# Second cross-attention: the key stack copied in two sides, its maxima found over four groups of a quad

## What is computed

```python
qn = layernorm(q, norm_w, norm_b)
kn = layernorm(k, norm_w, norm_b)
vn = layernorm(v, norm_w, norm_b)
Q = (qn @ Wq + bq).reshape(b, l, H, E)        # b 16, l 64, H 16 heads, E 16
K = (kn @ Wk + bk).reshape(b, s, H, E)        # s 1601
V = (vn @ Wv + bv).reshape(b, s, H, E)
scores = jnp.einsum('blhe,bshe->bhls', Q, K)
A = jax.nn.softmax(scale * scores, axis=-1)
O = jnp.einsum('bhls,bshd->blhd', A, V) + Q
```

## Time and profile before

| | before |
|---|---|
| median of three runs | 1640.6 us (1639.12 to 1641.78) |
| profiled execution | 1641.75 us, span 1640.0 us |
| PE, DVE, ACT, POOL busy | 88%, 61%, 40%, 39% of the span |
| mean granted clock of PE | 0.895 of full |
| the attention's 32 quads | about 582 to 1376 us of the span |

### The profile page before, as it was taken

One profiled execution on the slowest core, in us unless ns is written; L12 is line 12 of the kernel. 1 busy time (PEld: TensorE's weight loads), 2 busy tenths in 40 slices (PEclk: granted clock), 3 DMA queues, 4 the chain that ended last, 5 costly groups with the idle time before them and its releaser, 6 DMA issues. The chain is left out here.

```text
span 1640.0 us, 29797 instructions
## 1 busy us (share of the span) xinstructions
PE 1450.6 (88%) x11472; PEld 1148.9 (70%) x11472; DVE 995.0 (61%) x1896; ACT 655.0 (40%) x1268; POOL 641.6 (39%) x559
## 2 busy tenths in 40 slices
PE   6988877765994899999999999999999997489998
PEld 3655545444884678888888888888888875357787
DVE  4999964476236556666666666666665652644445
ACT  1444432131200455555545555545555533143322
POOL 0000000001001458777777777787776642222110
PEclk9877788866996899999999999999999985699999
DMA  9479700800142566766657767658666451311000
GB/s 358 157 276 326 266 2 1 298 2 0 59 148 89 139 159 164 188 158 161 158 144 180 173 158 168 150 144 197 169 150 143 98 109 26 107 39 64 0 1 27
DMA packets 109296, 219.61 MB, mean 134 GB/s; under 512 B 10871, under 2 KB 83095, under 8 KB 108391
## 3 DMA queue, kind: packets, MB, share of 16 engines
q1 hardware_dynamic: 109163, 217.80, 47.6%
HBM read 132.51 MB, written 6.40 MB: 85 GB/s over the span
## 5 line engine op out<-in xcount | busy, mean ns | idle before, releaser
L1905 DVE TENSOR_REDUCE d_top<-psum 128x1 f32<-128x400 f32 (+2 forms) x512 | 270.2, 569 | 97.7 <-PE psum L1549 90.5
L1449 POOL TENSOR_TENSOR d_ring<-d_ring 128x512 f32<-128x512 f32 x224 | 290.6, 1297 | 78.8 <-ACT d_ring L1734 61.1
L1734 ACT ACTIVATE d_ring<-psum 128x512 f32<-128x512 f32 (+1 forms) x416 | 229.2, 595 | 207.3 <-PE psum L1567 189.0
L1567 PEld LDWEIGHTS psum<-d_queries,d_stack 100*128 100x128 f32 (+1 forms) x1664 | 214.5, 198 | 36.7 <-issue 34.7
L1567 PE MATMUL psum<-d_queries,d_stack 100*128 100x128 f32 (+1 forms) x1664 | 235.9, 286 | 0.9 <-DVE d_queries L1920 0.9
L1549 PE MATMUL psum<-d_stack,d_queries 96*128 96x400 f32 (+1 forms) x512 | 171.8, 394 | 13.0 <-DVE d_top L1905 10.5
L1379 POOL TENSOR_TENSOR d_rowsT<-d_raw,d_rowsT 128x768 fp32r<-128x768 f32 (+2 forms) x62 | 118.2, 1908 | 156.2 <-ACT d_rowsT L1705 156.2
L1534 PE MATMUL psum<-d_wv,d_rowsT 128*128 128x256 f32 (+1 forms) x1248 | 169.9, 285 | 0.0
L1526 PE MATMUL psum<-d_rowsT,d_wk 128*128 128x384 f32 (+2 forms) x768 | 160.5, 358 | 3.5 <-POOL d_rowsT L1379 1.9
L1534 PEld LDWEIGHTS psum<-d_wv,d_rowsT 128*128 128x128 f32 (+1 forms) x1248 | 161.4, 187 | 0.5 <-issue 0.5
L973 POOL TENSOR_TENSOR c_partL<-moe_in,c_partH 128x256 fp32r<-128x256 f32 x8 | 5.5, 742 | 389.6 <-ACT c_partH L1061 389.6
(11 more groups left out here) (394 smaller groups left out, 2292.6 us busy)
## 6 DMA issues: line engine op xcount, KB each, us to landing
d_stack<-d_stage SPq DMA_DIRECT2D x384, 200.2 KB, 4.2
a_cR<-ctx_rows_dram SPq DMA_DIRECT2D x16, 1664.0 KB, 9.6
a_cT<-ctxT_dram SPq DMA_DIRECT2D x16, 1601.0 KB, 14.4
moe_w<-moe_w_dram SPq DMA_DIRECT2D x16, 1024.0 KB, 10.6
d_rowstd<-row_stds_dram SPq DMA_DIRECT2D x16, 801.0 KB, 5.5
d_raw<-ctxT_dram SPq DMA_DIRECT2D x32, 384.0 KB, 5.7
d_raw<-ctxT_dram SPq DMA_DIRECT2D x16, 512.0 KB, 6.0
d_queries<-queries_dram SPq DMA_DIRECT2D x96, 64.0 KB, 2.0
```

The source lines that it names most:

```text
L1449: pool.tensor_tensor(sums[:, 0, m, :], first, ring[:, slot_of(u, m, c), :], ALU.add)\
L1567: last = pe.matmul(ps[0:w, S_BANK + (m + c) % 2, j * P:(j + 1) * P], stack[0:STACKED, m, j, c * P:c * P + w], queries[0:STACKED, m, j, :], ...
L1734: act.activation(ring[0:w, slot_of(u, m, c), :], ps[0:w, S_BANK + (m + c) % 2, :], ACT.Exp)\
L1905: dve.tensor_reduce(top[:, m, v:v + 1], ps[:, M_BANK + v % 2, 0:min(w, S - s0)], X, ALU.max)\
```

## The change

The stack's copies are made in two sides: side 0 has the columns of chunks 0 to 6 (896 columns), side 1 the rest (706), with 12 copies each. Side 0 of a stack is copied as soon as the quad that still uses this stack is past chunk 6, while its side 1 is still read; side 1 and the queries come at that quad's end, as the whole stack did. The products of `find_top` are reordered: v = 0 to 7 are the two left units of all four j and need side 0 alone, v = 8 to 15 need side 1. Their places go from groups 2, 3, 4 (six, six, four) to groups 1 to 4: two at the end of group 1, then seven, five and four. `take_top` follows the same order. In SP's queue the loads of two quarters of rows stand behind the new copy of side 0, and in the prologue likewise.

```diff
-    TOP_AT = {2: (0, 6), 3: (6, 12), 4: (12, 16)}
+    TOP_AT = {1: ((), (), (0, 1)), 2: ((2, 3), (4, 5), (6,)), 3: ((7, 8), (9, 10), (11,)), 4: ((12, 13), (14, 15), ())}
+    SIDES, SPLIT = 2, 7
+    TOP_ORDER = [(j, 2 * h + i) for h in range(SIDES) for j in range(4) for i in range(2)]
...
-    FIRST_TOPS = {9: (0, 1), 10: (2, 3), 11: (4, 5, 6, 7), 12: (8, 9, 10, 11), 13: (12, 13), 14: (14, 15)}
+    FIRST_TOPS = {8: (0, 1, 2), 9: (3, 4), 10: (5, 6), 11: (7, 8, 9), 12: (10, 11), 13: (12, 13), 14: (14, 15)}
...
-            def load_stack(b, m):
+            def load_queries(b, m):
 
                 n = 2 * b + m
-                wait(sp, "d_lows", 4 * n + 4)
                 wait(sp, "d_s_ps", NC * (n - 1))
...
+            def load_side(b, m, h):
+
+                n = 2 * b + m
+                cols = slice(0, SPLIT * P) if h == 0 else slice(SPLIT * P, SE)
+                wait(sp, "d_lows", 4 * n + 2 * h + 2)
+                if n >= 2:
+                    wait(sp, "d_s_ps", NC * (n - 1) if h else NC * (n - 2) + SPLIT)
                 for j in range(4):
                     for part, r in ((0, 0), (1, 32), (0, 64)):
-                        sp.dma_start(stack[r:r + 32, m, j, :].bitcast(F32),
-                                     stage[32 * j:32 * j + 32, m, part, :].bitcast(F32))\
-                          .then_inc(sig(f"d_stack_in{m}{j}"), 16)
+                        sp.dma_start(stack[r:r + 32, m, j, cols].bitcast(F32),
+                                     stage[32 * j:32 * j + 32, m, part, cols].bitcast(F32))\
+                          .then_inc(sig(f"d_stack_in{m}{h}"), 16)
...
                 if now:
-                    load_stack(b, 1)
+                    load_queries(b, 1)
+                    load_side(b, 1, 1)
...
                 if after:
-                    load_stack(b + 1, 0)
+                    load_side(b + 1, 0, 0)
+                    load_queries(b + 1, 0)
+                    load_side(b + 1, 0, 1)
                     store_own(b + 1, 1)
                 if ahead:
                     load_stds(b + 3)
-                    for q in range(3):
+                    load_rows(b + 3, 0)
+                if after:
+                    load_side(b + 1, 1, 0)
+                if ahead:
+                    for q in range(1, 3):
                         load_rows(b + 3, q)
...
-                n, j = 2 * b + m, v // 4
-                s0, w = UNITS[v % 4]
+                n, (j, q) = 2 * b + m, TOP_ORDER[v]
+                s0, w = UNITS[q]
...
-                if v % 4 == 0:
-                    wait(pe, f"d_stack_in{m}{j}", 48 * (b + 1))
+                if v % 8 == 0:
+                    wait(pe, f"d_stack_in{m}{v // 8}", 192 * (b + 1))
...
-                        tops = list(range(*TOP_AT[g])) if ahead and g in TOP_AT else []
+                        tops = TOP_AT[g] if ahead and g in TOP_AT else ((), (), ())
                         for c in chunks:
                             score(b, u, m, c)
-                        for v in tops[0:2]:
+                        for v in tops[0]:
                             find_top(*nxt, v)
...
-                dve.tensor_reduce(top[:, m, v:v + 1], ps[:, M_BANK + v % 2, 0:min(w, S - s0)], X, ALU.max)\
+                dve.tensor_reduce(top[:, m, 4 * j + q:4 * j + q + 1], ps[:, M_BANK + v % 2, 0:min(w, S - s0)], X, ALU.max)\
...
-                            for v in range(*TOP_AT[g]):
+                            for v in sum(TOP_AT[g], ()):
                                 take_top(*nxt, v)
```

More of the change, by code:

```diff
@@ L1337, in _ @@
             load_stds(1)
-            for q in range(4):
+            for q in range(2):
                 load_rows(1, q)
-            load_stack(0, 0)
+            load_side(0, 0, 0)
+            for q in range(2, 4):
+                load_rows(1, q)
+            load_queries(0, 0)
+            load_side(0, 0, 1)
             store_own(0, 1)
@@ L1343, in _ @@
               .then_inc(sig("d_marks_in"), 16)
-            load_stack(0, 1)
+            load_side(0, 1, 0)
+            load_queries(0, 1)
+            load_side(0, 1, 1)
             store_own(1, 0)
@@ L1618, in batch @@
                                 fill(b + 1, 1 - u, n)
-                        for v in tops[2:4]:
+                        for v in tops[1]:
                             find_top(*nxt, v)
@@ L1629, in batch @@
                             denominators(*before(b, u, m)[::2])
-                        for v in tops[4:6]:
+                        for v in tops[2]:
                             find_top(*nxt, v)
@@ L1902, in take_top @@
                 n = 2 * b + m
-                s0, w = UNITS[v % 4]
+                j, q = TOP_ORDER[v]
+                s0, w = UNITS[q]
                 wait(dve, "d_top_ps", TOPS * n + v + 1)
-                dve.tensor_reduce(top[:, m, v:v + 1], ps[:, M_BANK + v % 2, 0:min(w, S - s0)], X, ALU.max)\
+                dve.tensor_reduce(top[:, m, 4 * j + q:4 * j + q + 1], ps[:, M_BANK + v % 2, 0:min(w, S - s0)], X, ALU.max)\
                    .then_inc(sig("d_top"), 1)
```

## The result

The changed kernel takes 1658.99 us (median of 4 runs, 1658.49 to 1659.68) against 1639.86 us for the kernel before (4 runs, 1636.55 to 1641.78): ratio 1.0119, 95% interval 1.0101 to 1.0137. It is 19 us slower. The profiled execution has a span of 1656.7 us, 16.7 us over that of before.

What follows compares the result with a forecast made beforehand. TensorE, busy 88% of the span, was taken to bound the kernel by its own order of work. +21 - 1.3 + 0 + 6 = +26 us on 1641.75 gave 1667.5, or 1666 us at the median; range 1648 to 1690, about 0.8.

Steps and rivals of the forecast that it cites:

- The new wait: Between groups 1 and 2, T2 and T3 wait for VectorE's takes 0 and 1: 1.2 to 1.3 us added per quad.
- The old waits: Six-product groups outrun VectorE in their last pair: 0.30 us in each of two groups, 0.6 us a quad removed.
- Net per quad: New wait less old waits in quads 0 to 29: +0.7 us each, bounds +0.5 and +0.85.
- What stays: Odd quads' group 4 without a fill keeps its four products and its wait at T14: costed at nothing.
- Copies: 24 smaller copies on SP's queue, 0.6 us each to issue, 7.2 us a side: hidden behind the quad's work.
- Quad 30: Quad without fills: T0's 1.29 us wait for the stack's copy goes, T8 may meet side 1: -1.3 us, bounds -3 and +2.
- The clock: TensorE's granted clock halves at waits, 3.0 us a fall: two more falls, +6 us, bounds none and ten.
- the prediction's own sign of being wrong: Falls of the clock in group 2 or 3 would count against the forecast and point to more falls.
- first rival: More clock falls at the new wait, 5 to 12 more: +15 to +36 us, 1675 to 1695 us, chance 0.25.
- The sum: All terms together: +26 us on the profiled execution, 1666 us at the median, own range 1657 to 1674.
- what lies ahead of quad 2: Prologue, two more takes ahead of its fills and the same work: 0, bounds -2 and +2; quads 0 and 1 count per quad.

Runs made afterwards that it cites:

- places_alone: Kernel before with only the products' places changed to the new groups, copies in one piece, old prologue: 1660.00 us, ratio 1.0134.
- before_heads5: Kernel before with take_heads moved from group 1 to group 5 of VectorE's order, nothing else: 1639.18 us, ratio 0.9986.
- sides_old_places: Changed kernel with the products back in their old groups and old prologue places, two-sided copies kept: 1638.65 us, ratio 0.9983.
- after_heads5: Changed kernel with take_heads moved from group 1 to group 5 of VectorE's order: 1627.17 us, ratio to before 0.993.
- heads5_fill4: after_heads5 with the odd quads' last value fill moved from group 5 to their empty group 4: 1611.74 us, ratio 0.9821.
- heads5_fill4_low5: heads5_fill4 with GpSimd's low part of the third quarter of rows moved from group 4 to 5 of odd quads: 1612.03 us, ratio 0.9846.

## Why the prediction was right, point by point

- **The new wait: right, in place and size.** "T2 starts 2.1 to 2.2 us after T0 with DVE named as releaser": 948.64 - 946.49 = 2.15 us. The fill starts 0.77 us behind T2, where 0.76 to 0.86 was worked out, and so 1.18 us later than without the wait (1.2 to 1.3 forecast). Its cause was shown by taking take_heads out of the chain in both kernels.
- **The old waits went**, 0.6 us a quad, as put: behind the weighing stands one product now, and none waits.
- **Net per quad: right.** +0.66 and +0.61 us against +0.7; even quads 25.57 (25.6 forecast), odd ones 24.39 (24.5). 30 quads at 0.64 are 19 us where 21 stood.
- **What stays: right.** The product pairs of the odd quads' group 4 were left as they were; covering them later took 0.72 us from an odd quad.
- **Copies: right in quads 0 to 29.** 8.0 to 8.2 us a side (7.2 forecast), no DMA ahead of T0 or T8, and with the old places the whole costs nothing. The rule of the Trainium skill to batch DMAs to a megabyte (DMA: Bandwidth & Descriptors, "Bandwidth") speaks of the share of the peak bandwidth; for the kernel's time it had no weight here, with copies of 88 to 112 KB that are hidden. What the Trainium skill says of copies within SBUF and small descriptors (same page, "Why small descriptors are slow (HBM only)") isn't contradicted: issue and landing both fell with the size, from 0.94 and 4.2 us to 0.59 and 2.3. The prediction didn't ask whether the one-piece copies would be early enough for the new places too; places_alone showed that they are, but for quad 30.
- **Quad 30: mis-sized, and for another reason.** -1.3 us was T0's wait. That is gone, but T8 now waits 1.08 us for side 1, which the prediction had named as possible and put into its bounds alone. It gave 2.6 us all the same, and 3.5 with the old places, as more of the quad ran at full clock (0.74 and 0.79 against 0.64).
- **The clock: wrong in the count and in the price.** Seven of ten falls in quads 2 to 29 begin in group 2 around the start of the value fill, some 11 us into quads 3, 11, 13, 18, 21, 23 and 25; three stay behind group 4 of quads 5, 19 and 27. Before there were five, four of them in these 28 quads. Falls in group 2 were the prediction's own sign of being wrong, and its first rival's count (5 to 12 more) is the one that came: six more, where two were put. But those in group 2 last 3.4 us and cost 1.5 (25.92 against 24.39 us in the rows above), not 3.0. So the term of +6 measured +4.4 in this stretch by luck: two errors nearly cancel. Nor is it a steady number: kernels whose products stand in the old places fell four times (before, before_heads5) and seven times (sides_old_places) in the same 28 quads.
- **The sum**: 1666 forecast, 1659 measured. Against the profile: waits 19 instead of 21 (17.8 of them in quads 2 to 29), quad 30 -2.6 instead of -1.3, clock +4.4 instead of +6, and what lies ahead of quad 2 -4.2 instead of 0, or -2.9 with the 1.3 us of waits that quads 0 and 1 have. Of the 4.2, 2.2 are gone before quad 0 starts, and 2.0 are the clock's in quads 0 and 1, of which 10.2 us ran at 1.2 GHz before and 3.4 us after. The start isn't the change's doing for certain: four kernels with the same prologue start quad 0 between 579.4 and 584.1 us.

## What to carry to other kernels

When a producer is moved earlier, look at where its consumer stands in the other engine's written order, and what has to run ahead of it there: two PSUM banks let the producer go two steps ahead, then it waits for that whole chain. Moving the chain's movable part away (here take_heads, free in group 5) turned the loss of 19 us into a gain of 13. Covering the bare group brought the lowest median, 1611.74 us, though by the clock and not by the quads' own length. A move that is worth nothing alone (before_heads5) can be what makes another one pay, so the two have to be tried together.

## What the runs showed of the hardware

The granted clock doesn't need a long stop of TensorE to fall to 1.2 GHz: from 640 to 1340 us of the kernel after, PE never waited longer than 0.7 us for VectorE. In quads 2 to 29 of each profiled execution it fell like this:

| kernels | PE idle ahead of | falls in group 2 | behind group 4 |
|---|---|---|---|
| before, before_heads5, sides_old_places | T14 (odd quads), 0.5 us | 0, 0, 0 | 4, 4, 7 |
| after, places_alone | T2 (all quads), 0.7 us, and T14 | 7, 9 | 3, 1 |
| after_heads5 | T14 | 0 | 3 |
| heads5_fill4 | second score (even quads), 0.77 us | 0 | 0 |
| heads5_fill4_low5 | T8 (some even quads), up to 0.6 us | 0 | 0 |

The falls stand at the waits of T2 and T14, and where such a wait is gone its falls are gone too. But idle time of the same length ahead of the second score brought none, so its length alone doesn't decide. With both waits covered the stretch is at full clock throughout:

```profile
632.00:1308.69 676.69, 665.20 (x7088) 567.53 (x7085) 483.72 (x785) 373.42 (x682) 510.26 (x445) 1.00 0.64 162
```

A fall in group 2, with a value fill behind it, lasted 3.4 us and cost 1.5. Behind the group without a fill it lasted 6.8 us and cost 3.0 in quad 9 of the kernel before, but 3.4 and 1.5 as well in the kernel with take_heads moved (quad 11: 24.96 instead of 23.44 us). One kernel can have both: before_heads5 has the short fall in quads 7 and 19 (25.34 us) and the long one in 13 and 25 (26.81 us). What sets the length stays open. The Trainium skill's "A second HAM failure mode: psum-queue depth-cycling" (TensorE: Matmul & The Clock Gate) tells of short idles between groups of matmuls that cycle through PSUM banks; the falls at T2 and T14 agree with it, and the runs add the prices.

Identical code elsewhere in the program moved by up to 5 us from kernel to kernel (behind the start of quad 31 it is 284.2 us in the kernels before and after, 279.4 in heads5_fill4), and the clock goes with it, as the two rows from quad 31 above show. That bounds how finely a single profile can be read.
